# Reordering the first loads and the lead-in of group 0 in a fused two-layer kernel (recurrent attention, gated feed-forward, cross-attention, ternary feed-forward)

## The chip, the cores and the metric

The kernel runs on one core of one Trainium2 chip. The metric is the device time of one execution in microseconds (us); lower is better. The engines are PE (TensorE matmul; PEld is its weight load), DVE (VectorE), ACT (ScalarE), POOL (GpSimd) and SP (SyncE, which here only issues DMAs). Each engine runs its own instructions in program order and waits on semaphores for the others. A name with a q behind it in the profile (SPq, ACTq, POOLq) is the engine's sequencer, which issues DMAs.

## The reference

Sixteen sequences of 128 rows by 256 features pass through four residual stages; the first one is what the change touches.

```python
x = x + mlstm(layernorm(x), ctx, ctx, igate_w, igate_b, fgate_w, fgate_b, ln_scale)   # stage A
x = x + swiglu_ffn(layernorm(x), w_gate, w_up, w_down)                                # stage B
x = x + cross_attention(layernorm(x), ctx, mask, W, diagonal)                         # stage C
x = x + ternary_ffn(layernorm(x), w1, w2, h1, h2, w3)                                 # stage D

def mlstm(q, k, v, ...):                       # 8 heads of 32 features
    ifg = concatenate([q, k, v], axis=-1)
    ig, fg = (ifg @ igate_w.T + igate_b).T, (ifg @ fgate_w.T + fgate_b).T
    cs = cumsum(log_sigmoid(fg), axis=1)
    log_D = where(tril, cs[:, :, None] - cs[:, None, :], -inf) + ig[:, None, :]
    max_log_D = max(log_D, axis=-1, keepdims=True)
    C = (q k^T per head / sqrt(32)) * exp(log_D - max_log_D)
    normalizer = maximum(abs(C.sum(-1)), exp(-max_log_D))
    h = (C / (normalizer + 1e-6)) @ v
    return layernorm(h over all 256 features) * ln_scale
```

## The kernel before, in words

The sixteen sequences are worked on in four groups of four (`G` = 4, `Q` = 4; a group has 512 rows, `GT`). Each engine has one hand-written program: the order of its instructions is the order of the source, and semaphores tie the programs together. Stage A is a loop over the groups in which each group has eight units (four sequences by two sets of four heads, the "quads"). Before the loop stands the lead-in of group 0, which is what the change reorders. Later groups have their own lead-in inside the loop, one group ahead; the loop body is untouched but for one wait.

The lead-in of group 0 goes as follows, by the names in the code.

- SP issues the loads: `x` (group 0, semaphore `x_first`), `graw` (the raw gate weights, `gw_ld`), `kstA` (the transposed context of group 0, `ctxT_ld`), `idf` (an identity matrix, `ident_ld`), small constants (`consts`), and `x` of group 1 (`x_second`).
- DVE computes the statistics of `x` (`x_stats`), POOL the inverse root of the variance (`inv_root`, line 412, semaphore `rstd_ready`), DVE the normalised `xn` (`x_norm`, line 1096). PE transposes `xn` into PSUM (`turn_x`, line 558). Each f32 operand is then split into a rounded high part and a rest: ACT writes the high part of `xT` (`x_hi`, line 889) and of `kT` (`k_hi`, line 893), DVE the low parts (`x_lo`, line 1103, and its own `k_lo`, line 1108). POOL has a `k_lo` as well (line 431), which the loop and the later stages use.
- POOL clears `gw`, `Qb` and `V` (memsets, lines 404 to 408) and builds the split gate weights `gw` from `graw` (lines 417 to 425, semaphore `gw_lo`). `gsum` is the sum of the weights for k and for v.
- PE computes the gates (`gates`, lines 564 to 566, twelve matmuls of 512 columns: six from `kT`, which wait for `klo_done` and `gw_lo`, then six from `xT`). ACT copies them to `gsb` (`gate_copy`, line 897, semaphore `gate_copied`). Two DMAs bring them into `gi` and `gf`, one row per head and sequence.
- DVE and ACT form log-sigmoid, running sum, running minimum and the three bf16 pieces `zp` of the result (`gate_a`, ACT's `log_part`, `gate_b`, ACT's `floor_part`, `gate_c`; semaphore `z_ready` at line 1148). Six DMAs move the pieces into the rows of `Rr` and `Lr`; each adds 16 to `z_moved`.
- The loop on PE opens with `expo` (line 603), which waits for all six (`MOVES` = 96), then `qk` with `Qb`, which SP fills from `xT` (`queries_in`, line 283, four DMAs for each sequence). `V` is filled by four DMAs (`values`, line 273) after the memsets have counted `const_set` to 3. POOL's weight loads for stage B (line 439 on) wait for `z_moved` too.

In the kernel before, SP issues `V`, then `gi`, `Qb`, `x` of groups 2 and 3 and the three `Rr` moves, while ACT issues `gf` and the three `Lr` moves. Line 244 and 245 (`move_rows`) are the form that the loop uses for the later groups, where SP issues all six:

```python
def move_rows(sp, u):
    for part in range(3):
        sp.dma_start(Rr[part:part + 1, u, :, :, :, :], zp[:, part, 0, :]).then_inc(s["z_moved"], 16)
        sp.dma_start(Lr[3 + part * Q:3 + part * Q + Q, u, :, :, :], zp[:, part, 1, :])\
            .then_inc(s["z_moved"], 16)
```

Of the kernel before, what the change touches and what calls it, by code (L numbers as in the profile page):

```python
# [24 lines left out]
NH, DH = 8, 32  # L25
KD = D // P
Q = 4
G = NB // Q
GT = Q * S
# [31 lines left out]
class Chain:  # L61
# [5 lines left out]
    def step(self, ins):  # L67
        ins.then_inc(self.sem, 1)
        self.n += 1
# [18 lines left out]
def two_layers(nc, x_in, ctx_in, ctxT_in, mask_in, gw_in, gb_in, lns_in, l0gu_in, l0d_in, xaw_in, diag_in,  # L88
# [17 lines left out]
    with es:  # L106
# [145 lines left out]
        def _(sp):  # L252
            sp.dma_start(x[:, 0:Q, :], x_in[0:Q].rearrange("b s d -> s b d")).then_inc(s["x_first"], 16)
            sp.dma_start(graw[:, :, :], gw_in).then_inc(s["gw_ld"], 16)
            sp.dma_start(kstA[:, :, :], ctxT_in[:, :, 0:GT]).then_inc(ctxT_ld[0], 16)
            sp.dma_start(idf[:, :], ident_in).then_inc(s["ident_ld"], 16)
            sp.dma_start(gb[:, :], gb_in).then_inc(s["consts"], 16)
# [4 lines left out]
            sp.dma_start(tri[:, :, :], tri_in).then_inc(s["consts"], 16)  # L262
            sp.dma_start(x[:, Q:2 * Q, :], x_in[Q:2 * Q].rearrange("b s d -> s b d")).then_inc(s["x_second"], 16)
            sp.dma_start(lns[:, :], lns_in.partition_broadcast(P)).then_inc(s["consts"], 16)
# [4 lines left out]
            sp.dma_start(kstA[:, :, :], ctxT_in[:, :, GT:2 * GT]).then_inc(ctxT_ld[1], 16)  # L269

            def values(g, u):
                for q in range(Q):
                    sp.dma_start(V[:, u, q, 0:NH, 0:DH],
                                 ctx_in[Q * g + q].rearrange("t (h d) -> t h d", d=DH)).then_inc(v_ld[u], 16)
# [26 lines left out]

            sp.wait_ge(s["const_set"], 3)
            values(0, 0)
            sp.wait_ge(s["gate_copied"], 1)
            sp.dma_start(gi[:, :], gsb[0:NH, :].rearrange("h (q t) -> h q t", q=Q)).then_inc(s["gate_moved"], 16)
            queries_in(0, 0, 0)
            for g in range(2, G):
                sp.dma_start(x[:, Q * g:Q * g + Q, :], x_in[Q * g:Q * g + Q].rearrange("b s d -> s b d"))\
                    .then_inc(s["x_rest"], 16)
            sp.wait_ge(s["z_ready"], 1)  # L310
            for part in range(3):
                sp.dma_start(Rr[part:part + 1, 0, :, :, :, :], zp[:, part, 0, :]).then_inc(s["z_moved"], 16)
            queries_in(0, 0, 1)
            with sp.Fori(0, 2) as i:
# [79 lines left out]
        def _(pool):  # L394
            own = [0]

            def step(ins):
                ins.then_inc(s["pool_own"], 1)
                own[0] += 1

            def settle():
                pool.wait_ge(s["pool_own"], own[0])
# [4 lines left out]

            nc.gpsimd.memset(V[:, :, :, :, :], 1.0).then_inc(s["const_set"], 1)

# [3 lines left out]

            settle()
            inv_root(0)
            pool.wait_ge(s["gw_ld"], 16)
            step(nc.gpsimd.tensor_tensor(gsum[:, :, :], graw[:, KD:2 * KD, :], graw[:, 2 * KD:3 * KD, :], ALU.add))
            settle()
            W = 2 * NH
# [8 lines left out]
            def k_lo(n, kst, u):  # L428
# [3 lines left out]
                    .then_inc(s["klo_done"], 1)  # L432

            inv_root(1)
            pool.wait_ge(s["z_moved"], MOVES)

# [442 lines left out]
        def _(act):  # L879
# [45 lines left out]
            gate_copy(0, QK)  # L925
            act.wait_ge(s["gate_copied"], 1)
            act.dma_start(gf[:, :], gsb[NH:2 * NH, :].rearrange("h (q t) -> h q t", q=Q)).then_inc(s["gate_moved"], 16)
            k_hi(1, kstA[:, :, :], 1)
            x_hi(1, 1)
            log_part(0)  # L930
            floor_part(0)
            act.wait_ge(s["z_ready"], 1)
            for part in range(3):
                act.dma_start(Lr[3 + part * Q:3 + part * Q + Q, 0, :, :, :], zp[:, part, 1, :])\
                    .then_inc(s["z_moved"], 16)
            with act.Fori(0, 2) as i:
# [128 lines left out]
        def _(dve):  # L1065
# [39 lines left out]

            def k_lo(n, par):
                dve.wait_ge(s["khi_done"], n + 1)
                v.tensor_tensor(kT[:, par, 1, :, :], kstA[:, :, :], kT[:, par, 0, :, :], ALU.subtract)\
                    .then_inc(s["klo_done"], 1)

            A2 = 9
# [114 lines left out]
            v.tensor_copy(idb[:, :], idf[:, :]).then_inc(s["idb_ready"], 1)  # L1226
            k_lo(0, 0)
            x_lo(0, 0)
# [7 lines left out]
            x_lo(1, 1)  # L1236
            k_lo(1, 1)
            floor_copy(0, 0)
            with dve.Fori(0, 2) as i:
                for u in range(2):  # L1240
# [6 lines left out]
                    for q in range(Q):  # L1247
# [3 lines left out]
                        if q == 0:  # L1251
                            def close():
                                finish(last, 1 - u, Q - 1, norm=True)
                            before(close)

                            if u == 0:
                                dve.wait_ge(s["pv_used"], Q * g + 1)
                                dve.wait_ge(s["x_rest"], 16 * (G - 2))
                                x_stats(g + 2, 8 - 8 * i)
                            else:  # L1260
                                more(lambda: x_stats(3, 3 * Q))
# [232 lines left out]
```

## Time and profile before

| what | us |
|---|---|
| median of 3 runs | 616.87 (616.14 to 617.22) |
| the profiled execution | 617.22 |
| its span in the trace | 615.7 |
| PE busy | 557.8 (91%) |
| DVE busy | 352.0 (57%) |
| ACT busy | 213.9 (35%) |
| POOL busy | 89.0 (14%) |
| first matmul of stage A's loop | 28.55 after the start |

All times of a row are counted from the start of the span. A timeline row has the start, the length, the engine and line, what it writes and reads, and in brackets how long the engine had been idle before it and what ended that idle time. Where a row merges several instructions, xN is their count and the length is from the first's start to the last's end. A row that tells "DMA to landing" counts from the issue of a DMA to the moment at which its data has landed and its semaphore says so.

### The profile page before, as it was taken

To read this page: it belongs to the slowest core of one execution; us is meant where nothing else is said; L and a number is where in the kernel's file an instruction comes from. 1 tells how busy PE (TensorE), PEld (TensorE's weight loads), DVE (VectorE), ACT (ScalarE), POOL (GpSimd) and SP (SyncE) were. 2 spreads that over 40 slices of the span, in tenths; PEclk is the share of its full clock that TensorE was granted. 3 is DMA by queue.
4 is the path that set the end of the run, shared out by engine and by line. 5 is a ranking of instruction groups with operands and counts; after the bars stand their busy time and mean duration, and the time that the engine had idled before them with its cause. 6 is when DMAs were issued, how large, how long until landed. Compare 5 with 4: busy or idle time off the path is not lost.

```text
span 615.7 us, 8969 instructions
## 1 busy us (share of the span) xinstructions
PE 557.8 (91%) x2728; PEld 452.8 (74%) x2728; DVE 352.0 (57%) x853; ACT 213.9 (35%) x372; POOL 89.0 (14%) x110
## 2 busy tenths in 40 slices
PE   3397988887899999979999999999999999999994
PEld 3164665566788887757888888888878888888884
DVE  6468899877777777865424345344363434542232
ACT  2223142242666663334411236112162222441120
POOL 5114343233300023310000010000100000100001
PEclk9588979886899999988999999999999999999998
DMA  7565444525954739830000000000000000000000
GB/s 202 123 164 150 105 118 78 140 85 189 341 215 149 192 70 353 175 96 1 1 0 2 0 35 1 0 2 0 27 9 0 0 0 0 34 0 0 0 0 34
DMA packets 57752, 47.57 MB, mean 77 GB/s; under 512 B 37278, under 2 KB 48542, under 8 KB 57316
## 3 DMA queue, kind: packets, MB, share of 16 engines
q1 hardware_dynamic: 51960, 28.29, 17.8%
q0 software_dynamic: 5616, 18.88, 9.3%
q8 instruction: 15, 0.25, 0.2%
q14 instruction: 13, 0.11, 0.1%
q10 hardware_dynamic: 148, 0.04, 0.0%
HBM read 40.58 MB, written 2.10 MB: 69 GB/s over the span
## 4 chain that ended last, share of the span: by engine, by line
PE 69%; DVE 4%; issue 2%; ACT 2%; DVEq 0%; POOL 0%; ACTq 0%; POOLq 0%
PE ps L794 52%; PE ps L570 6%; PE ps L573 3%; PE ps L572 2%; PE ps L558 2%; DVE xn L1096 1%; PE ps L765 1%; PE ps L564 1%; ACT al L1024 1%; PE ps L566 1%; PE ps L565 1%; PE ps L779 1%; PE ps L626 0%; ACT h L1059 0%; DVE sc L1344 0%
## 5 line engine op out<-in xcount | busy, mean ns | idle before, releaser
L794 PE MATMUL ps<-hBt,h 128*128 128x512 f32 x512 | 117.4, 390 | 0.0
L794 PE MATMUL ps<-hA,h 128*128 128x512 f32 x512 | 117.2, 390 | 0.0
L794 PEld LDWEIGHTS ps<-hA,h 128*128 128x128 f32 x512 | 95.9, 188 | 20.2 <-DVE hA L1390 0.4
L794 PEld LDWEIGHTS ps<-hBt,h 128*128 128x128 f32 x512 | 95.8, 188 | 20.2 <-DVE hBt L1390 0.4
L1059 ACT ACTIVATE h<-ps,scol 128x512 f32<-128x512 f32 x64 | 44.1, 690 | 175.4 <-PE ps L794 175.3
L794 PE MATMUL ps<-xT,w 128*128 128x512 f32 x256 | 60.7, 397 | 0.2 <-issue 0.2
L794 PEld LDWEIGHTS ps<-xT,w 128*128 128x128 f32 x256 | 46.8, 190 | 13.4 <-DVE h L1385 2.5
L1405 DVE CAST hBt<-h 128x512 fp32r<-128x512 f32 x32 | 13.7, 427 | 73.7 <-ACT h L1059 73.7
L1405 DVE CAST hA<-h 128x512 fp32r<-128x512 f32 x32 | 13.7, 427 | 70.1 <-ACT h L1059 70.1
L412 POOL TENSOR_TENSOR rstd<-ve,mhalf 128x4 f32<-128x4 f32 x16 | 16.4, 1023 | 251.0 <-DVE ve L1091 251.0
L570 PE MATMUL ps<-xT,l 128*128 128x512 f32 x96 | 40.5, 421 | 4.7 <-issue 2.7
L573 PE MATMUL ps<-xT,l 128*128 128x512 f32 x96 | 40.0, 416 | 0.0
L1044 ACT ACTIVATE silD<-ps,scol 128x512 f32<-128x512 f32 x32 | 22.0, 688 | 50.6 <-PE ps L794 50.6
L1385 DVE SCALAR_TENSOR_TENSOR h<-ps,scol,silD 128x512 f32<-128x512 f32 x32 | 24.0, 751 | 24.0 <-ACT silD L1044 24.0
L539 POOL DMA_DIRECT2D out<-x x16 | 8.8, 553 | 178.1 <-DVE x L1416 178.1
L558 PE MATMUL ps<-idf,xn 128*128 128x128 f32 x128 | 18.9, 296 | 14.3 <-DVE xn L1096 14.3
L946 ACT ACTIVATE Dt<-ps 128x512 f32<-128x512 f32 x32 | 19.0, 595 | 35.1 <-PE ps L605 33.8
L1096 DVE TENSOR_SCALAR xn<-x,mv,rstd 128x256 f32 (+1 forms) x64 | 27.1, 486 | 5.0 <-POOL rstd L412 4.7
L889 ACT ACTIVATE xT<-ps 128x512 fp32r<-128x512 f32 x32 | 17.3, 593 | 35.4 <-PE ps L558 35.4
L558 PEld LDWEIGHTS ps<-idf,xn 128*128 128x128 f32 x128 | 16.1, 153 | 17.3 <-DMA idf<-ident_in 9.3
L570 PEld LDWEIGHTS ps<-xT,l 128*128 128x128 f32 x96 | 19.6, 204 | 10.0 <-issue 3.0
L570 PE MATMUL ps<-l0d,hB 128*128 128x256 f32 x96 | 24.1, 291 | 1.4 <-DVE x L1315 1.4
(170 smaller groups left out, 931.5 us busy)
## 6 DMA issues: line engine op xcount, KB each, us to landing
looked<-w_all_in SPq DMA_DIRECT2D x16, 704.0 KB, 4.8
h<-w_all_in POOLq DMA_DIRECT2D x16, 512.0 KB, 6.4
V<-ctx_in SPq DMA_DIRECT2D x32, 128.0 KB, 4.4
Qb<-xT SPq DMA_DIRECT2D x64, 64.0 KB, 2.4
w<-w_all_in POOLq DMA_DIRECT2D x3, 1024.0 KB, 6.9
x<-x_in SPq DMA_DIRECT2D x4, 512.0 KB, 4.3
kstA<-ctxT_in SPq DMA_DIRECT2D x4, 512.0 KB, 5.3
kstC<-ctxT_in SPq DMA_DIRECT2D x4, 512.0 KB, 5.5
```

Of the source, the lines that this page charges most:

```text
L412: nc.gpsimd.tensor_tensor(rstd[:, :], ve[:, :], mhalf[:, :], ALU.pow).then_inc(s["rstd_ready"], 1)
L558: last = nc.tensor.transpose(ps[:, TR + c, q * S:(q + 1) * S], xn[:, q, c * P:(c + 1) * P], idf[:, :])
L570: mm(o, lhs(0), rhs(0), start=first, stop=False)
L573: return mm(o, lhs(0), rhs(1), start=False, stop=last)
L794: last = mm(o, a, b, start=(k == 0 and p == 0), stop=(k == n_k - 1 and p == 1))
L889: fn(xT[:, par, 0, c, :], tr_bank(c), ACT.Copy).then_inc(s["xhi_done"], 1)
L946: fn(Dt[:, quad, :, :], ps[:, EX + quad, :].rearrange("p (j t) -> p j t", j=Q), ACT.Exp, scale=-1.0).then_inc(s["d_ready"], 1)
L1044: fn(silD[:, m % 2, :], ps[:, 2 + m % 2, :], ACT.Silu, scale=scol[:, 0, m:m + 1])\
L1059: fn(h32[:, m % 2, :], ps[:, 2 + m % 4, :], ACT.Gelu, scale=scol[:, L + 1, m:m + 1])\
L1096: last = v.tensor_scalar(xn[:, q, :], x[:, b0 + q, :], mv[:, q, 0:1], rstd[:, q:q + 1], ALU.subtract, ALU.mult)
L1385: v.scalar_tensor_tensor(out=h32[:, m % 2, :], in0=ps[:, 4 + m % 2, :], scalar=scol[:, 1, m:m + 1], in1=silD[:, m % 2, :], op0=ALU.mult, o ...
L1405: v.tensor_copy(dst[:, 0, m, :], h32[:, m % 2, :]).then_inc(s["dh_own"], 1)
```

## The change

The line numbers of the changed kernel are a little lower, since it is shorter. What it does:

- SP's first loads are in another order: `x`, `idf`, `kstA`, `graw`, `x` of group 1, then the constants.
- POOL adds up `gsum` (which needs `graw`) ahead of the first `inv_root`. It computes the low parts of `kT` for groups 0 and 1, which DVE did; the memset of `V` stands between the two.
- SP's lead-in of group 0 uses the loop's own helpers: `gi` and `gf` together, then `x` of groups 2 and 3, then `V`, `Qb`, and all six moves. It waits for `const_set` ahead of `gi`. ACT issues no DMA any more.
- On ACT, `log_part(0)` stands ahead of the `x_hi` of group 1.
- DVE waits for `x_rest` once ahead of the loop, not in it.

```diff
@@ sync (SP)
             sp.dma_start(x[:, 0:Q, :], x_in[0:Q].rearrange("b s d -> s b d")).then_inc(s["x_first"], 16)
+            sp.dma_start(idf[:, :], ident_in).then_inc(s["ident_ld"], 16)
+            sp.dma_start(kstA[:, :, :], ctxT_in[:, :, 0:GT]).then_inc(ctxT_ld[0], 16)
             sp.dma_start(graw[:, :, :], gw_in).then_inc(s["gw_ld"], 16)
-            sp.dma_start(kstA[:, :, :], ctxT_in[:, :, 0:GT]).then_inc(ctxT_ld[0], 16)
-            sp.dma_start(idf[:, :], ident_in).then_inc(s["ident_ld"], 16)
+            sp.dma_start(x[:, Q:2 * Q, :], x_in[Q:2 * Q].rearrange("b s d -> s b d")).then_inc(s["x_second"], 16)
             sp.dma_start(gb[:, :], gb_in).then_inc(s["consts"], 16)
...
-            sp.dma_start(x[:, Q:2 * Q, :], x_in[Q:2 * Q].rearrange("b s d -> s b d")).then_inc(s["x_second"], 16)
...
-
+            sp.wait_ge(s["const_set"], 3)
...
-            sp.wait_ge(s["const_set"], 3)
-            values(0, 0)
-            sp.wait_ge(s["gate_copied"], 1)
-            sp.dma_start(gi[:, :], gsb[0:NH, :].rearrange("h (q t) -> h q t", q=Q)).then_inc(s["gate_moved"], 16)
-            queries_in(0, 0, 0)
+            gates_in(0)
             for g in range(2, G):
                 sp.dma_start(x[:, Q * g:Q * g + Q, :], x_in[Q * g:Q * g + Q].rearrange("b s d -> s b d"))\
                     .then_inc(s["x_rest"], 16)
-            sp.wait_ge(s["z_ready"], 1)
-            for part in range(3):
-                sp.dma_start(Rr[part:part + 1, 0, :, :, :, :], zp[:, part, 0, :]).then_inc(s["z_moved"], 16)
-            queries_in(0, 0, 1)
+            lead_in(0, 0)
@@ gpsimd (POOL)
-            nc.gpsimd.memset(V[:, :, :, :, :], 1.0).then_inc(s["const_set"], 1)
+            pool.wait_ge(s["gw_ld"], 16)
+            step(nc.gpsimd.tensor_tensor(gsum[:, :, :], graw[:, KD:2 * KD, :], graw[:, 2 * KD:3 * KD, :], ALU.add))
+            settle()
...
-            settle()
             inv_root(0)
-            pool.wait_ge(s["gw_ld"], 16)
-            step(nc.gpsimd.tensor_tensor(gsum[:, :, :], graw[:, KD:2 * KD, :], graw[:, 2 * KD:3 * KD, :], ALU.add))
-            settle()
...
+            k_lo(0, kstA[:, :, :], 0)
+            nc.gpsimd.memset(V[:, :, :, :, :], 1.0).then_inc(s["const_set"], 1)
             inv_root(1)
+            k_lo(1, kstA[:, :, :], 1)
             pool.wait_ge(s["z_moved"], MOVES)
@@ scalar (ACT)
             gate_copy(0, QK)
-            act.wait_ge(s["gate_copied"], 1)
-            act.dma_start(gf[:, :], gsb[NH:2 * NH, :].rearrange("h (q t) -> h q t", q=Q)).then_inc(s["gate_moved"], 16)
             k_hi(1, kstA[:, :, :], 1)
+            log_part(0)
             x_hi(1, 1)
-            log_part(0)
             floor_part(0)
-            act.wait_ge(s["z_ready"], 1)
-            for part in range(3):
-                act.dma_start(Lr[3 + part * Q:3 + part * Q + Q, 0, :, :, :], zp[:, part, 1, :])\
-                    .then_inc(s["z_moved"], 16)
@@ vector (DVE)
-            k_lo(0, 0)
             x_lo(0, 0)
...
-            k_lo(1, 1)
             floor_copy(0, 0)
+            dve.wait_ge(s["x_rest"], 16 * (G - 2))
...
-                                dve.wait_ge(s["x_rest"], 16 * (G - 2))
```

On SP, from the second load of `kstA` to the moves of the pieces, before the change (a name on the left of the arrow is written, one on the right is read; L is the line, xN a count):

```order
L269 DMA kstA<-ctxT_in 128x2x512 [waits klo_done]
L273 DMA V<-ctx_in 128x8x32 [waits const_set]
L273 DMA V<-ctx_in 128x8x32 x3
L305 DMA gi<-gsb 32x1x128 [waits gate_copied]
L283 DMA Qb<-xT 32x4x128 [waits qk_done,xhi_done,xlo_done]
L283 DMA Qb<-xT 32x4x128 x3
L308 DMA x<-x_in 128x4x256 x2
L312 DMA Rr<-zp 1x32x128 [waits z_ready]
L312 DMA Rr<-zp 1x32x128 x2
```

The same stretch of SP after the change:

```order
L269 DMA kstA<-ctxT_in 128x2x512 [waits klo_done]
L290 DMA gi<-gsb 32x1x128 [waits gate_copied,const_set]
L291 DMA gf<-gsb 32x1x128
L304 DMA x<-x_in 128x4x256 x2
L273 DMA V<-ctx_in 128x8x32 x4
L283 DMA Qb<-xT 32x4x128 [waits qk_done,xhi_done,xlo_done]
L283 DMA Qb<-xT 32x4x128 x3
L244 DMA Rr<-zp 1x32x128 [waits z_ready]
L245 DMA Lr<-zp 4x8x128
L244 DMA Rr<-zp 1x32x128
L245 DMA Lr<-zp 4x8x128
L244 DMA Rr<-zp 1x32x128
```

Four `V` loads that stood ahead of the wait for `gate_copied` now stand behind it, and four moves more (`gf` and the three `Lr`) are SP's; the last `Lr` follows the twelfth row.

On POOL, from the last memsets to the second inverse root, before the change:

```order
L406 MEMSET Qb 128x2048
L408 MEMSET V 128x2640
L412 ISA
L412 TENSOR_TENSOR rstd<-ve,mhalf 128x4 [waits mv_ready,pool_own]
L417 TENSOR_TENSOR gsum<-graw 128x32 [waits gw_ld]
L420 CAST gw<-graw 128x2x16 [waits pool_own]
L421 CAST gw<-gsum 128x2x16
L423 TENSOR_TENSOR gw<-graw,gw 128x2x16 [waits pool_own]
L425 TENSOR_TENSOR gw<-gsum,gw 128x2x16
L412 TENSOR_TENSOR rstd<-ve,mhalf 128x4 [waits mv_ready]
```

The same stretch of POOL after the change:

```order
L399 MEMSET Qb 128x2048
L402 ISA
L402 TENSOR_TENSOR gsum<-graw 128x32 [waits gw_ld]
L407 TENSOR_TENSOR rstd<-ve,mhalf 128x4 [waits mv_ready,pool_own]
L411 CAST gw<-graw 128x2x16
L412 CAST gw<-gsum 128x2x16
L414 TENSOR_TENSOR gw<-graw,gw 128x2x16 [waits pool_own]
L416 TENSOR_TENSOR gw<-gsum,gw 128x2x16
L422 TENSOR_TENSOR kT<-kstA,kT 128x1024 [waits khi_done]
L426 MEMSET V 128x2640
L407 TENSOR_TENSOR rstd<-ve,mhalf 128x4 [waits mv_ready]
L422 TENSOR_TENSOR kT<-kstA,kT 128x1024 [waits khi_done]
```

The wait for the load of `graw` moved ahead of the first inverse root, and two subtractions of 128 by 1024 for `kT` were added.

## Rows read from the trace of the kernel before

**Rows 1.** Waits from 0 to 30 us: total us, times, longest
```profile
POOL l L439 <- DMA Lr<-zp: 12.3, 1, 12.3
```

**Rows 2.** Timeline, 2.7 to 16 us: start, length, engine, line [idle before]
```profile
2.75 0.59 SPq L256 DMA_DIRECT2D idf<-ident_in  x1
...
6.77 1.04 POOL L412 TENSOR_TENSOR rstd<-ve,mhalf 128x4 f32<-128x4 f32 x1 [0.81 <-DVE ve L1091]
...
7.79 0.24 POOL L417 TENSOR_TENSOR gsum<-graw 128x32 f32<-128x32 f32 x1
7.84 1.38 DVE L1096 TENSOR_SCALAR xn<-x,mv,rstd 128x256 f32<-128x256 f32 x4 [1.23 <-POOL rstd L412]
...
8.72 0.28 POOL L423 TENSOR_TENSOR gw<-graw,gw 128x32 fp32r<-128x32 f32 x1
8.97 1.63 POOL L425 TENSOR_TENSOR gw<-gsum,gw 128x32 fp32r<-128x32 f32 x1
...
9.27 1.22 DVE L1108 TENSOR_TENSOR kT<-kstA,kT 128x1024 fp32r<-128x1024 f32 x1
...
10.96 0.78 PE L564 MATMUL ps<-kT,gw 128*128 128x512 f32 x1
...
15.63 0.59 ACT L897 ACTIVATE gsb<-ps 16x512 f32<-16x512 f32 x1 [3.20 <-PE ps L566]
```

**Rows 3.** DMA issues from 0 to 40 us: count, KB each, median us to landing
```profile
idf<-ident_in SPq DMA_DIRECT2D x1, 64.0 KB, 5.8
graw<-gw_in SPq DMA_DIRECT2D x1, 48.0 KB, 3.1
```

**Rows 4.** POOL's own k_lo in the loop, line 431: min/median/max ns
```profile
L431 POOL TENSOR_TENSOR kT<-kstA,kT x2: 2365/2370/2374, 60.2 to 89.6; 128x1024 fp32r<-128x1024 f32 x2
```

**Rows 5.** Timeline of the sequencers and the loop's first matmul, 10 to 29 us
```profile
10.52 0.56 SPq L269 DMA_DIRECT2D kstA<-ctxT_in  x1
...
11.12 3.95 SPq L273 DMA_DIRECT2D V<-ctx_in  x4
...
16.24 0.86 SPq L305 DMA_DIRECT2D gi<-gsb  x1
...
17.23 2.61 SPq L283 DMA_DIRECT2D Qb<-xT  x4
...
19.89 1.54 SPq L308 DMA_DIRECT2D x<-x_in  x2
...
25.07 2.04 ACTq L934 DMA_DIRECT2D Lr<-zp  x3
...
28.55 0.60 PE L603 MATMUL ps<-Rr,Lr 15*128 15x512 bf16 x1 [1.82 <-DMA Lr<-zp]
```

**Rows 6.** The third of the four V issues alone, timeline of SP
```profile
12.49 1.88 SPq L273 DMA_DIRECT2D V<-ctx_in  x1
```

**Rows 7.** Landing of line 269 (kstA), then of line 308 (x): min/median/max
```profile
DMA to landing us min/median/max: 4.0/4.0/4.0
...
DMA to landing us min/median/max: 3.6/4.3/5.0
```

**Rows 8.** Timeline in the loop, group 1, where SP issues everything
```profile
50.16 0.56 SPq L244 DMA_DIRECT2D Rr<-zp  x1
...
53.84 0.68 SPq L245 DMA_DIRECT2D Lr<-zp  x1
```

**Rows 9.** Timeline, the gate chain of group 0 on DVE and ACT
```profile
18.78 0.28 DVE L1116 TENSOR_SCALAR fmn<-gf,gb 32x128 f32<-32x128 f32 x1 [0.97 <-DMA gf<-gsb]
...
20.85 0.29 ACT L902 ACTIVATE fl<-fab 32x128 f32<-32x128 f32 x1
```

**Rows 10.** Timeline in the loop, POOL and DVE side by side
```profile
45.10 1.79 POOL L454 TENSOR_TENSOR l<-rawgu,l  x1
45.23 1.80 DVE L1138 TENSOR_TENSOR Er<-Z,cs 32x128 f32<-32x128 f32 x1
```

**Rows 11.** Windows, 28.5 to 35 us: busy of each engine, PE's granted clock, DMA
```profile
28.50:35.00 6.50, 6.45 (x15) 3.99 (x16) 2.34 (x6) 1.19 (x2) 2.35 (x4) 0.50 0.88 265
```

More of the change, by code:

```diff
@@ L1104, in x_lo @@
                         .then_inc(s["xlo_done"], 1)
[L1106 to L1109, printed above, removed]
             A2 = 9
```

## The prediction, made before the changed kernel ran

> **What bounds the kernel now.** I read the waits of the first 30 us, then the timeline up to the loop's first matmul, then the DMA landings. PE carries the kernel from the loop's opening on, and the loop opens at 28.55, when the last `Lr` move has landed [rows 5]. POOL's weight loads for stage B wait for the same moves, 12.3 us [rows 1], and every later load waits for work of the loop or behind it. So nothing behind the opening runs by a time of its own: a shift of the opening shifts the end by as much. The change leaves the loop body alone; the whole question is when the loop opens.
>
> Three points lie on the way to it. R is the end of the first inverse root: 6.77 + 1.04 = 7.81. T is the end of the gate copy: 15.63 + 0.59 = 16.22. The opening comes 28.55 - 16.22 = 12.33 after T [rows 2, 5].
>
> **R: the wait for graw stands ahead of the root.** POOL now needs `graw` before the root. `graw` is issued fourth, in the place that `idf` had: issue at 2.75, behind the 512 KB of `kstA`. `idf` landed 5.8 later, at 8.55; `graw`, second in line before, landed after 3.1 [rows 2, 3]. By the place in the queue it lands at 8.55; the sum of the weights (0.24) and the root (1.04) then give R = 9.9 with the gaps: **+2.1**. If it kept its 3.1 it would land at 5.9, before the statistics are ready at 6.77, and R would not move: the other end is 0. I take 2.1, since the size is like that of `idf` (48 and 64 KB) and the place is the same. The Trainium skill, "DMA: Bandwidth & Descriptors", section "Queues, rings and completion order", says that each DMA engine consumes the descriptors of one ring in order, though a later one may finish its write first; the row of `idf` agrees with the first half, and by the second half alone the term could be nearer to 0.
>
> **From R to T: the low part of kT on POOL.** Before, PE started the gates at 10.96, which is R + 3.15: DVE's `k_lo` took 1.22 and ran beside POOL's work on `gw`. Now POOL does both in a row. Its own `k_lo` takes 2.37 [rows 4] and can't start before the `gw` splits are through. From R to the start of the last split were 8.97 - 7.81 = 1.16, less 0.24 for the sum, which has gone ahead: 0.92. The last split took 1.63 where its twin took 0.28, and it ended at 10.60, just behind DVE's `k_lo` (9.27 to 10.49) [rows 2]. I read it as held up by DVE, so with that work gone it costs 0.28, once DVE's `xn` is through at R + 1.41. Then: R + 1.44 + 0.28 + 2.37 + 0.36 (10.60 to 10.96, release to matmul) = R + 4.45, or **+1.3**. Ends: 0.92 + 0.28 + 2.37 + 0.36 = 3.93, +0.8; and with 1.63 as the split's own price 0.92 + 1.63 + 2.37 + 0.36 = 5.28, +2.1. The Trainium skill, "SBUF — State Buffer", section "SBUF: two separate sides", has VectorE and GpSimd share a pair of ports as an exclusive lock, which a VectorE instruction with two SBUF inputs takes against a GpSimd one; the pair 0.28 and 1.63 agrees. By that rule the term is 1.3, and without it 2.1.
>
> The `xT` side is no later than that: it moves with R and is ready at 13.3 + 2.1 = 15.4, when PE is still at its six `kT` matmuls (from 14.3 on). I leave the twelve matmuls and the way to the copy at 15.63 - 10.96 = 4.67. T comes at 16.22 + 2.1 + 1.3 = 19.6, **+3.4**.
>
> **From T to the opening: SP's queue.** Two things have to be there: `z_ready`, and SP. `z_ready` gains. It came at 25.05, T + 8.8. ACT's exp ran at 20.85 behind `x_hi(1)`, though `fab` had been ready at about 19.4 [rows 9]; `log_part` now stands ahead: -1.5. `gf` goes behind `gi` on SP, 0.86 + 0.68 against 1.33 on ACT's queue: +0.2. That makes T + 7.6.
>
> SP is later. From T it issues `gi` 0.86, `gf` 0.68 (the price of a move of the same queue [rows 8]), `x` twice 1.54, `V` 3.95 and `Qb` 2.61 [rows 5]: T + 9.65. Only `gi`, `Qb` and `x` stood there before, and `V` was issued from 11.12 to 15.07, where SP had nothing else to do. The `V` price may grow. Three of the four issues are near 0.66, and the third took 1.88, up to 14.37 [rows 6], which is when the 512 KB of `kstA` that stood ahead (10.52 + 4.0) landed [rows 5, 7]. Now 1 MB of `x` stands ahead: its second half, issued at about T + 2.3, lands at T + 7.3 by the 5.0 of [rows 7]. If the third `V` issue is again held till then, the fourth and `Qb` bring SP to T + 7.3 + 0.66 + 2.61 = T + 10.6. Without any stall it is T + 8.4. I take T + 10.2, between the row as it stands and the longer one.
>
> Then all six moves go out from one queue, where ACT and SP shared them (ACT's three took 2.04). In the loop the six span 50.16 to 54.52, 4.36, of which their own durations are about 3.7 [rows 8]; I take 4.0. The last lands 28.55 - 27.11 = 1.44 later [rows 5]. The opening is at T + 10.2 + 4.0 + 1.44 = T + 15.6, **+3.3** against 12.33. Ends: T + 8.4 + 3.7 + 1.44 = 13.5, +1.2; T + 10.6 + 4.4 + 1.44 = 16.4, +4.1, and 1.5 more if a second `V` issue is held.
>
> **What costs nothing, and its cover.** The memset of `V` (2.3) is behind `k_lo(0)` and ends near 16.5, before T. The second root waits for it, and `xn` of group 1 is done by about 20; it is wanted only for `x_lo(1)`, behind the gate chain. The second load of `kstA` is issued at 14 instead of 10.5 and lands at 18, before T. DVE loses its second `k_lo`, 1.2, which was off the way; POOL's second one, 2.4 from about T + 1.1, may hold the gate chain: in the loop a 32 by 128 instruction of DVE took 1.80 beside POOL's 1.79 [rows 10], where others of its size take 0.28 [rows 9]. SP's slack of 10.2 - 7.6 = 2.6 covers that; without the slack it would cost up to 1.5. The wait for `x_rest` on DVE is met at about T + 7.3, before DVE gets there. Behind the opening all stands as before: `Qb` of the second sequence follows the moves, and `V` lands long before its first use.
>
> **Sum.** 2.1 + 1.3 + 3.3 = 6.7. The profiled execution took 617.22 (span 615.7 and 1.5 around it), so it would take 623.9. The median of the three is 0.35 lower: **623.6**.
>
> **Rivals.**
> (a) `graw` lands early. For it: its 3.1 of before. Against: the row of `idf`. 6.7 - 2.1 = 4.6: 621.5.
> (b) SP is not what the opening waits for; the gate chain is. It decides where SP is through `Qb` by T + 7.6, which asks for issues 2 us shorter than those of [rows 5]. T + 7.6 + 4.0 + 1.44 = T + 13.0, +0.7; with 3.4 it gives 4.1: 621.0. With (a) too: 618.9.
> (c) The queues stall more: several `V` issues are held behind 1 MB of `x`, or the moves land late behind 4,096 small `V` rows and `Qb`, and the last split costs 1.63. 2.1 + 2.1 + 4.1 + 1.5 = 9.8: 626.7.
> (d) The opening is not what sets the end: some later transfer, started by a time of its own, ends the slack. I find none; it would give 616.9.
> (e) Faster: PE's clock. It is granted half speed in the first 6.5 us of the loop, with PE busy for 6.45 [rows 11]. Were it at full speed from the opening, these would take half, -3.2; with the least shift of the lead-in (0 + 0.8 + 1.2 = 2.0) that is -1.2: 615.7. It decides at a granted clock of 1.0 at the opening. Against it: PE has been idle ahead of the opening, as before, and for longer.
>
> **Chances and range.** A run of this kernel can tell about 0.2%, 1.2 us, from no change. My forecast with terms near their values 0.50; (a) 0.17; (b), with or without (a), 0.11; (c) 0.14; (d) 0.04; (e) 0.04. Slower by over 0.2% are the first four but for a rest of (b) with (a): 0.90. Within it: 0.06. Faster: 0.04. The range goes from 619.3, above the case of (a) with (b), to 626.8, where (c) is taken in.
>
> **What would show it.** POOL's `gsum` at about 8.6 and the root's end near 9.9 (step one; at 6.1 and 7.8 it is wrong). POOL's `k_lo` ending near 14, with a last split of 0.3, PE's first gate matmul at 14.3 (step two). The gate copy ending at 19.6. The third `V` issue stalled till `x` lands, `z_ready` 2 us before SP takes it, six moves in 4 us, and the loop's first matmul near 35.2 (step three). From there on the same distance to the end, 587 us. I would be wrong altogether if that distance changed by over 1 us.

## The result, and the profile after

The changed kernel took 621.88 us (median of 6 runs, 620.58 to 624.29) against 616.5 for the kernel before (614.6 to 617.51, 6 runs). The ratio is 1.0109, with a 95% interval from 1.0078 to 1.0141: about 1% slower. It rests on more runs than the two medians do (22 of the changed kernel, whose median is 623.0), so it is not their quotient. All ratios leave out executions over 1.5% longer than the shortest of the same kernel; for a_guard and a_fix these are five of before's 19. The span of the profiled execution went from 615.7 to 622.1, +6.4. The forecast was 623.6, +6.7. The sum was close, but not by its own steps: the loop opened 9.5 later, not 6.7, and the loop gave 3.1 back, which I had forecast at nothing.

The first view is the timeline of the changed kernel, POOL, DVE and the first gate matmul, in the stretch that [rows 2] shows of before (start, length, engine, line, operands, idle before):

```profile
9.53 0.24 POOL L402 TENSOR_TENSOR gsum<-graw 128x32 f32<-128x32 f32 x1 [5.82 <-DMA graw<-gw_in]
9.86 1.04 POOL L407 TENSOR_TENSOR rstd<-ve,mhalf 128x4 f32<-128x4 f32 x1
...
10.93 3.43 DVE L1084 TENSOR_SCALAR xn<-x,mv,rstd 128x256 f32<-128x256 f32 x4 [4.32 <-POOL rstd L407]
...
11.50 0.30 POOL L416 TENSOR_TENSOR gw<-gsum,gw 128x32 fp32r<-128x32 f32 x1
11.76 2.45 POOL L422 TENSOR_TENSOR kT<-kstA,kT 128x1024 fp32r<-128x1024 f32 x1
14.16 2.44 POOL L426 MEMSET V<- 128x2640 f32 x1
...
14.28 2.40 DVE L1209 CAST idb<-idf 128x128 bf16<-128x128 f32 x1
...
16.78 0.77 PE L558 MATMUL ps<-kT,gw 128*128 128x512 f32 x1 [0.33 <-issue]
...
21.59 0.59 ACT L891 ACTIVATE gsb<-ps 16x512 f32<-16x512 f32 x1 [4.01 <-PE ps L560]
```

Two things are to be seen. POOL waits 5.82 for `graw`, and the root ends at 10.90 instead of 7.81. Then `xn`, four instructions of DVE, takes 3.43 instead of 1.38, and the cast of `idb` 2.40 instead of 0.2. Both end just when an instruction of POOL does: `xn` at 14.36 behind `k_lo` (14.21), the cast at 16.68 behind the memset (16.60). One line of the source view shows that one of the four instructions took all of it (min, median, max in ns):

```profile
L1084 DVE TENSOR_SCALAR xn<-x,mv,rstd x4: 399/421/2424, 10.9 to 11.9; 128x256 f32<-128x256 f32 x4
```

The landing of `graw`, from the view of DMA issues that [rows 3] shows of before:

```profile
graw<-gw_in SPq DMA_DIRECT2D x1, 48.0 KB, 6.7
```

The second stretch goes from the gate copy (T = 22.18) to the opening of the loop, on SP and DVE, as [rows 5, 6, 9] do of before:

```profile
23.93 0.99 SPq L304 DMA_DIRECT2D x<-x_in  x2
24.97 4.96 SPq L273 DMA_DIRECT2D V<-ctx_in  x4
...
29.76 0.41 DVE L1131 TENSOR_TENSOR zp<-zr,zp 32x256 bf16<-32x256 f32 x1
30.04 2.74 SPq L283 DMA_DIRECT2D Qb<-xT  x4
...
32.82 0.60 SPq L244 DMA_DIRECT2D Rr<-zp  x1
...
36.08 0.67 SPq L245 DMA_DIRECT2D Lr<-zp  x1
...
38.07 0.60 PE L597 MATMUL ps<-Rr,Lr 15*128 15x512 bf16 x1 [6.20 <-DMA Lr<-zp]
```

`zp` is ready at 30.17, T + 8.0, and SP is through `Qb` at 32.78, T + 10.6: the moves wait for SP, not for their data. The third `V` issue alone, from the timeline of SP, took 2.40. It ended at 28.75, and the second half of `x`, issued at 24.42, landed 4.5 later, at 28.9:

```profile
26.35 2.40 SPq L273 DMA_DIRECT2D V<-ctx_in  x1
```

The third stretch is the opening of group 1. First before (the last move, issued at 53.84, is in [rows 8]), then after the change: SP's last moves, POOL's first weight load, and PE's first matmul of the group.

```profile
53.23 0.56 SPq L244 DMA_DIRECT2D Rr<-zp  x1
53.74 0.72 POOL L439 DMA_DIRECT2D l<-l0gu_in  x1
...
57.80 0.38 PE L603 MATMUL ps<-Rr,Lr 15*128 15x512 bf16 x1 [2.30 <-DMA Lr<-zp]
```

```profile
62.39 0.54 SPq L244 DMA_DIRECT2D Rr<-zp  x1
...
62.97 0.67 SPq L245 DMA_DIRECT2D Lr<-zp  x1
63.30 0.72 POOL L433 DMA_DIRECT2D l<-l0gu_in  x1
...
64.98 0.39 PE L597 MATMUL ps<-Rr,Lr 15*128 15x512 bf16 x1
```

Before, POOL's load was issued 0.10 ahead of the last move, that move landed about 3.3 after its issue had ended, and PE waited 2.30. After, the move was issued 0.33 ahead of the load, and PE did not wait. The windows around it show what followed (busy of PE, PEld, DVE, ACT, POOL, then PE's granted clock, DMA share and GB/s), before and after:

```profile
57.80:66.50 8.70, 8.70 (x38) 6.29 (x38) 5.67 (x18) 2.14 (x3) 3.12 (x3) 0.80 0.73 219
```

```profile
65.00:72.50 7.50, 7.45 (x39) 5.28 (x38) 7.11 (x22) 3.00 (x5) 3.55 (x4) 1.00 0.80 246
```

Behind the wait PE had a granted clock of 0.80 on average, without it 1.00, over nearly the same matmuls. So 2.3 came back at the opening of group 1 and 1.2 in the first two units behind it (9.5 late at the loop's opening, 7.2 at that of group 1, 6.0 two units further). At the later units the changed kernel is mostly 6.0 to 6.5 behind (7.6 at the most), and at the end of the span 6.4.

### The profile page after: what moved, and what is told of

It is laid out like the page before. It is cut to its first block, busy times and chain, and to the rows that moved or that the text cites. A ratio compares the mean times of both kernels' runs of the same rounds, so it can differ in the third digit from the quotient of the medians.

```text
span 622.1 us, 8968 instructions
## 1 busy us (share of the span) xinstructions
PE 555.4 (89%) x2728; PEld 449.4 (72%) x2728; DVE 354.3 (57%) x851; ACT 213.4 (34%) x372; POOL 92.4 (15%) x112
## 4 chain that ended last, share of the span: by engine, by line
PE 67%; DVE 3%; issue 2%; ACT 1%; POOL 0%; DVEq 0%; ACTq 0%; POOLq 0%
PE ps L788 51%; PE ps L564 5%; PE ps L567 3%; PE ps L566 2%; PE ps L552 2%; DVE xn L1084 1%; PE ps L759 1%; PE ps L558 1%; PE ps L560 1%; ACT al L1012 1%; PE ps L559 1%; PE ps L773 1%; ACT h L1047 0%; DVE sc L1325 0%; DVE x L1296 0%
## 5 line engine op out<-in xcount | busy, mean ns | idle before, releaser
L1084 DVE TENSOR_SCALAR xn<-x,mv,rstd 128x256 f32 (+1 forms) x64 | 29.2, 518 | 7.8 <-POOL rstd L407 7.8
```

Of the source, the lines that this page charges most:

```text
L1084: last = v.tensor_scalar(xn[:, q, :], x[:, b0 + q, :], mv[:, q, 0:1], rstd[:, q:q + 1], ALU.subtract, ALU.mult)
```

## The experiments

An opening is read from one profile each. It is told as a distance, since the first landings and PE's clock moved the gate copy of the five kernels with before's loads and POOL from 16.07 to 17.37, and what lies behind stage A varied by 6.6 between profiles (482.4 and 482.5 in before and after, 479.4 to 486.0 in others). R is the end of the first root, T the end of the gate copy. Each ratio is to the runs of before that were taken with that kernel, whose medians were 616.5 to 617.6. The profile of a_split is of an execution of 624.79, 5.5 above its median, so only its lead-in and the distance to group 1 are read.

| kernel | R | gates start - R | T | opening - T | group 1 - opening | total, median | ratio to before |
|---|---|---|---|---|---|---|---|
| before | 7.81 | 3.15 | 16.22 | 12.33 | 29.25 | 616.5 | |
| after | 10.90 | 5.88 | 22.18 | 15.89 | 26.91 | 621.88 | 1.0109 (1.0078 to 1.0141) |
| a_graw | 7.81 | 4.27 | 17.62 | 16.07 | 26.89 | 620.67 | 1.0047 (1.0021 to 1.0074) |
| a_klo_dve | 11.25 | 5.34 | 21.50 | 15.98 | 27.19 | 622.03, one run | |
| a_vmem | 10.26 | 5.20 | 20.10 | 15.89 | 27.06 | 621.59, one run | |
| a_split | 11.30 | 5.88 | 22.18 | 13.06 | 29.36 | 619.32 | 1.0044 (1.0013 to 1.0075) |
| a_vfirst | 9.79 | 5.88 | 21.31 | 13.22 | 26.68 | 618.13, one run | |
| a_guard | 10.26 | 7.44 | 22.35 | 15.89 | 27.09 | 618.73 | 1.0072 (1.003 to 1.0115) |
| a_fix | 7.86 | 4.76 | 18.65 | 13.23 | 26.93 | 613.04 | 0.9985 (0.9935 to 1.0036) |
| b_onequeue | 7.82 | 4.71 | 17.19 | 13.33 | 26.81 | 612.24, one run | |
| b_log | 7.81 | 3.52 | 16.70 | 10.90 | 28.70 | 615.63 | 0.9978 (0.9942 to 1.0013) |
| b_guard | 7.81 | 4.09 | 16.07 | 11.95 | 27.28 | 611.85 | 0.9927 (0.9897 to 0.9957) |
| b_both | 7.81 | 4.85 | 17.37 | 11.15 | 28.39 | 611.54 | 0.9902 (0.9869 to 0.9935) |

The column "gates start - R" says something of before itself. Up to the gates its program is that of b_onequeue, b_log, b_guard and b_both, and yet it has 3.15 where they have 3.52 to 4.85: in them `idf` landed 6.4 to 7.8 after its issue, and `kstA` 6.8 to 8.1, instead of 5.8 and 6.0. So before's profile shows its lead-in at the fast end, and against those four the way from R to T grew by 1.7 to 3.0, not by 2.9.

**POOL's work holds up DVE: three runs.** The first moves `graw` ahead, so that `xn` is over when POOL's long instructions begin.

```diff
             sp.dma_start(x[:, 0:Q, :], ...)
-            sp.dma_start(idf[:, :], ident_in)...
-            sp.dma_start(kstA[:, :, :], ctxT_in[:, :, 0:GT])...
             sp.dma_start(graw[:, :, :], gw_in)...
+            sp.dma_start(kstA[:, :, :], ctxT_in[:, :, 0:GT])...
+            sp.dma_start(idf[:, :], ident_in)...
```

> The changed kernel with graw issued second again and idf fourth. Theory 1 (two terms: graw's place in the queue, and POOL's work in SBUF holding up DVE): the root ends at 7.8 instead of 10.9, xn then runs from 7.8 to 9.2, ahead of POOL's k_lo, which starts when k_hi is through at about 10.2, so xn takes 1.4 and not 3.4; the gates start near 12.9, the gate copy ends near 18.3, the loop opens at 34.2 instead of 38.07 (-3.9). Rival (xn was long for another reason, such as the loads landing beside it): only graw's own 3.1 comes back, the loop opens near 35.0 and xn stays at 3.4. Total near 618.

Its timeline:

```profile
6.77 1.04 POOL L407 TENSOR_TENSOR rstd<-ve,mhalf 128x4 f32<-128x4 f32 x1 [1.82 <-DVE ve L1079]
...
7.84 1.41 DVE L1084 TENSOR_SCALAR xn<-x,mv,rstd 128x256 f32<-128x256 f32 x4 [1.22 <-POOL rstd L407]
...
9.18 0.21 DVE L1209 CAST idb<-idf 128x128 bf16<-128x128 f32 x1
...
9.59 2.35 POOL L422 TENSOR_TENSOR kT<-kstA,kT 128x1024 fp32r<-128x1024 f32 x1 [0.87 <-ACT kT L887]
11.88 2.30 POOL L426 MEMSET V<- 128x2640 f32 x1
```

Every point came out as the first theory had it: the root at 7.81, `xn` 1.41, the gate copy at 17.62 (18.3 was expected), the opening at 33.69 (34.2). The late `graw` costs its own 3.1 and, through the place in which it puts `xn`, 1.6 more between R and the gates (5.88 to 4.27). The total is 620.67, ratio 1.0047 where the changed kernel had 1.0109: about 3.8 of the 4.4 by which the opening came sooner, as far as these intervals tell (they nearly touch).

The second takes `k_lo` from POOL and leaves the memset of `V` where the change put it.

```diff
@@ gpsimd
-            k_lo(0, kstA[:, :, :], 0)
             nc.gpsimd.memset(V[:, :, :, :, :], 1.0)...
             inv_root(1)
-            k_lo(1, kstA[:, :, :], 1)
@@ vector
+            k_lo(0, 0)      # behind the cast of idb, as before
+            k_lo(1, 1)      # behind x_lo(1, 1), as before
```

> The changed kernel with both k_lo of the lead-in back on DVE; POOL's memset of V stays where it is, so that it now follows the gw splits at once (about 11.8 to 14.2). Theory 1 (POOL's work in SBUF holds up DVE, a memset too): xn still takes about 3.4 and the gate copy still ends at 21.5 to 22.2. Rival (what cost was the length of POOL's k_lo in the chain of the gates): xn takes 1.4, the gates start 2.7 earlier, the gate copy ends near 19.5.

```profile
11.28 3.57 DVE L1082 TENSOR_SCALAR xn<-x,mv,rstd 128x256 f32<-128x256 f32 x4 [4.67 <-POOL rstd L407]
...
12.10 2.29 POOL L425 MEMSET V<- 128x2640 f32 x1
...
14.78 0.21 DVE L1212 CAST idb<-idf 128x128 bf16<-128x128 f32 x1
```

With no `k_lo` on POOL at all `xn` still takes 3.57, and its long instruction (2.57) ends at 14.5, behind a memset now. So the length of POOL's subtraction in the chain of the gates, which my step priced, was not what cost.

The third puts only the memset back ahead of everything.

```diff
             nc.gpsimd.memset(Qb[:, 0, :, :, :, :].bitcast(F32), 0.0)...
+            nc.gpsimd.memset(V[:, :, :, :, :], 1.0).then_inc(s["const_set"], 1)
             pool.wait_ge(s["gw_ld"], 16)
...
             k_lo(0, kstA[:, :, :], 0)
-            nc.gpsimd.memset(V[:, :, :, :, :], 1.0).then_inc(s["const_set"], 1)
```

> The changed kernel with the memset of V ahead of everything, as before the change. Theory 1: xn is still held by POOL's k_lo (3.4), but the cast of idb is not held by the memset (0.2 instead of 2.4), so the gates start 0.7 earlier, at 16.1, and the gate copy ends at 21.5 instead of 22.2. Rival (the cast was long for its own reasons): no change, 22.2.

```profile
10.29 3.43 DVE L1084 TENSOR_SCALAR xn<-x,mv,rstd 128x256 f32<-128x256 f32 x4 [3.67 <-POOL rstd L408]
...
11.13 2.45 POOL L423 TENSOR_TENSOR kT<-kstA,kT 128x1024 fp32r<-128x1024 f32 x1
13.65 0.21 DVE L1209 CAST idb<-idf 128x128 bf16<-128x128 f32 x1
```

`xn` as long as ever behind `k_lo`, the cast back at 0.21, the gates 0.7 sooner against R (5.20 against 5.88), as expected. T came 1.4 sooner than that, 20.10: `graw` had landed 0.6 earlier in this execution, and the gates ran at the higher clock sooner.

These three settle it: 2.05 for `xn` and 0.7 for the cast make up the 2.7 between R and the gates. The other profiles agree: `xn` took 3.43 to 5.67 in all six with `graw` fourth, and 1.38 or 1.41 in all seven with it second. The page of the Trainium skill that I cited, "SBUF — State Buffer", section "SBUF: two separate sides", names both sorts of VectorE instruction that take the shared ports, those with two SBUF inputs and those in a two-port performance mode. The traces agree with the second half, which I had left out: `xn` and the cast have one SBUF input each, and were held to the end of POOL's instruction. No trace shows the mode in which an instruction ran, and not every one was held: DVE's statistics of `x` took 1.33 beside the early memset of `V` in before and 1.33 without it in the changed kernel, and `x_lo`, which reads PSUM, took 1.29 beside the memset in a_graw and 1.29 in before.

**SP's queue behind the gate copy: three runs.** The first gives the lead-in of group 0 its old division back.

```diff
@@ sync
+            values(0, 0)          # ahead of the wait for gate_copied
+            ... gi, queries_in(0, 0, 0), x of groups 2 and 3, three Rr moves, queries_in(0, 0, 1)
-            gates_in(0)
-            ... x of groups 2 and 3
-            lead_in(0, 0)
@@ scalar
+            ... gf behind gate_copy(0), three Lr moves behind floor_part(0)
```

> The changed kernel with the lead-in of group 0 dealt out to SP and ACT as before the change (V ahead of the wait for the gate copy, gf and the three Lr moves on ACT); loads, POOL and the place of log_part as changed. Theory 2 (SP's queue sets the opening): the gate copy ends at 22.2 as in the changed kernel, z_ready is at T + 7.4, the moves leave in 2.0, the loop opens at T + 10.9 = 33.1 instead of T + 15.9. Rival (the landing of x and V sets it, not the issuing): it opens within 1 us of 38. For the total the opening is 5 earlier, so 616.9 if nothing is given back in the loop, 619 to 620 if what the loop gave back (3.1 at the opening of group 1) belongs to the late opening.

The opening came at T + 13.06, not T + 10.9, and not T + 15.9 either. SP's queue is 2.8 of the way, and something new took 2.1 of what was expected:

```profile
24.73 2.34 POOL L428 TENSOR_TENSOR kT<-kstA,kT 128x1024 fp32r<-128x1024 f32 x1 [2.78 <-ACT kT L893]
24.74 2.40 DVE L1111 TENSOR_SCALAR fmn<-gf,gb 32x128 f32<-32x128 f32 x1 [1.37 <-DMA gf<-gsb]
```

POOL's second `k_lo` started 0.01 ahead of the first instruction of the gate chain and held it for 2.40 instead of 0.28. The prediction had this case, at up to 1.5, under the cover of SP's slack. In the changed kernel the cover held (`fmn` 0.32 at 25.30); here, with SP ready, it had gone. The total is 619.32, where 619 to 620 was expected for the case that the late opening is what makes the loop give back; b_guard, below, shows that it is not. Group 1 opened 29.36 behind the loop, as in the kernel before: nothing was given back.

The second run moves only the `V` loads ahead of the wait and leaves all moves on SP.

```diff
+            values(0, 0)
             gates_in(0)
             ... x of groups 2 and 3
-            lead_in(0, 0)
+            queries_in(0, 0, 0)
+            sp.wait_ge(s["z_ready"], 1)
+            move_rows(sp, 0)
+            queries_in(0, 0, 1)
```

> The changed kernel with the four V loads ahead of the wait for the gate copy on SP, all six moves still on SP. Theory 2 in its parts: SP is through Qb at about T + 6, z_ready at T + 7.6 decides, the moves leave in 3.9 and land 1.4 later, so the loop opens at T + 12.9, 3.0 earlier against T than in the changed kernel (T + 15.9), and of the 3.6 that the lead-in grew behind T the V loads are 3.0 and the moves the rest. Rival (the second half of x, not V, holds SP and the moves): it opens at T + 15 or later.

```profile
15.52 2.93 SPq L273 DMA_DIRECT2D V<-ctx_in  x4
...
34.53 0.60 PE L601 MATMUL ps<-Rr,Lr 15*128 15x512 bf16 x1 [3.53 <-DMA Lr<-zp]
```

The opening is at T + 13.22 (12.9 expected). `V` behind the gate copy costs 2.7. Issued ahead of the gate copy, 1.8 after the 512 KB of `kstA` had been issued, the four take 2.93 and none is held.

The third starts from the kernel before and moves only `gf` and the three `Lr` moves to SP.

```diff
@@ sync
             sp.dma_start(gi[:, :], ...)
+            sp.dma_start(gf[:, :], ...)
...
                 sp.dma_start(Rr[part:part + 1, 0, :, :, :, :], ...)
+                sp.dma_start(Lr[3 + part * Q:3 + part * Q + Q, 0, :, :, :], ...)
@@ scalar
-            ... gf and the three Lr moves
```

> The kernel before with gf and the three Lr moves issued by SP, all else as before: the price of one queue alone. Theory 2: the six moves leave in 3.9 instead of 2.04 and gf lands about as before, so the loop opens 1.9 later, at 30.4. Rival (the landing sets the opening, not the issuing): 28.6.

```profile
30.52 0.60 PE L606 MATMUL ps<-Rr,Lr 15*128 15x512 bf16 x1 [3.56 <-DMA Lr<-zp]
...
57.33 0.39 PE L606 MATMUL ps<-Rr,Lr 15*128 15x512 bf16 x1
```

The opening came at 30.52 (30.4 expected), but 1.0 of it is a later T. Against T it is 13.33, +1.0: the moves take 3.9 instead of 2.0, and the chain ahead of them is 0.7 shorter, since ACT does not stand in the issue of `gf` (`z_ready` at T + 8.1 instead of T + 8.8). What I had not expected is group 1: it opened 26.81 behind the loop, and PE had no wait for `Lr`. With the kernel before's loads and POOL, 2.4 came back. So this part of the change costs 1.0 at the opening and brings more: its one run took 612.24, less than each of the 29 runs of before beside it (612.93 to 622.26), and in its profile the last unit of stage A starts 4.2 sooner than in before's.

**What the loop gave back: five runs.** Four of them try the order of the last move and POOL's loads. The guard is one wait more, in the loop of POOL:

```diff
                     if u == 0:
+                        pool.wait_ge(s["z_moved"], MOVES * (gn + 1))
                         pieces(i, 1)
                     else:
                         with pool.If(i < 1):
+                            pool.wait_ge(s["z_moved"], MOVES * (gn + 1))
                             pieces(1, 0)
```

> The kernel before with one wait more: in the loop POOL issues its weight loads for stage B only when the six moves of the next group have landed. Theory 3 (the last Lr move lands late since POOL's loads are already in the DMA engines; PE waits 2.3 for it at the opening of group 1 and then loses about 1 more at the half clock): group 1 opens at about 55.5 instead of 57.80 and the fourth unit behind it is 3.4 earlier; the loop's opening stays at 28.55. Total 3 lower, 614. Rival (the late opening of the changed kernel is what gave the 3 back, by other loads being through): no gain, group 1 opens at 57.8.

```profile
52.92 0.68 SPq L245 DMA_DIRECT2D Lr<-zp  x1
53.73 2.57 SPq L283 DMA_DIRECT2D Qb<-xT  x4
...
55.30 0.38 PE L605 MATMUL ps<-Rr,Lr 15*128 15x512 bf16 x1 [0.73 <-DMA Lr<-zp]
55.88 0.62 POOL L439 DMA_DIRECT2D l<-l0gu_in  x1 [3.01 <-DMA Lr<-zp]
```

Group 1 opened at 55.30 (55.5 expected); PE's wait fell from 2.30 to 0.73, the distance from 29.25 to 27.28, and from the second unit behind it on the units start 3.7 sooner (3.4 expected; 0.5 of it was there at the loop's opening). The total is 611.85, 0.9927 of before (0.9897 to 0.9957), more than the 3 expected. The rival, that the give-back belongs to the late opening, falls: here the loop opened early and the time came back too.

Why did the last move leave 0.4 later, and so behind POOL's load, in some kernels? In all profiles with before's SP program (before, a_split, b_log, b_guard, b_both) SP leaves 0.45 empty between the fourth and the fifth move of group 1; in all with a longer one (the changed kernel and the rest of its family that keep six moves on SP, b_onequeue) it does not. Nothing that the profile shows ends that gap. So the give-back goes with the length of SP's program, which the change happened to raise by four DMA issues; what makes the gap itself stays open.

The next run is the one part of the change that should gain, alone.

```diff
-            x_hi(1, 1)
             log_part(0)
+            x_hi(1, 1)
```

> The kernel before with log_part(0) ahead of x_hi(1) on ACT, alone. Theory: the exp runs at 19.4 instead of 20.85, z_ready and the moves come 1.5 earlier, the loop opens at 27.1. Rival (x_hi(1), now later, holds x_lo(1) and with it the opening): 28.5 or more. Total 1.5 lower if nothing in the loop takes it back.

The opening is at T + 10.90 instead of 12.33: 1.4 of the 1.5. The total is 615.63, ratio 0.9978 (0.9942 to 1.0013), which the timing can't tell from no change. Its profile has one thing more. PE waited 1.91 at group 1, and the windows behind that wait show the full clock, where before's showed 0.80:

```profile
56.30:64.00 7.70, 7.70 (x40) 5.66 (x41) 6.59 (x17) 2.42 (x4) 3.14 (x3) 1.00 0.66 201
```

So only the wait itself was lost there. Then both together:

> The kernel before with both: log_part first and POOL's loads behind the moves. If the two gains are apart and both hold, 4.5 to 5 lower than before, 612.5; the loop opens at 27.1 and group 1 at 54. Rival (stage A gives one of them back at a later group): 614 to 616.

The total is 611.54, ratio 0.9902 (0.9869 to 0.9935): the best of this study, by a little, and ahead of both kernels. Its interval overlaps with that of the guard alone. The loop opened at 28.52 and group 1 at 56.91, where 27.1 and 54 were expected. T was 1.15 later than in before, at 17.37, and against T the opening kept its gain (11.15). The distance to group 1 is 28.39, less than half of the guard's gain there; in this execution PE's granted clock was 0.61 in the 4.5 ahead of group 1 (its sixteen `V` matmuls there took 3.71, against 2.02 in the changed kernel).

> The changed kernel with POOL's loads in the loop behind the moves, as in b_guard. Theory 3: at group 1 there is nothing to win, since the moves land in time there already (distance from the loop's opening to that of group 1 stays at 26.9), but the late Qb landing of group 3 (between 120 and 135 us) goes, about 5. Total 617. Rival (the changed kernel has no such wait left): 622.

The changed kernel with the guard: 618.73 (617 expected), ratio 1.0072 (1.003 to 1.0115). That interval overlaps with the changed kernel's own. The distance to group 1 stays (27.09), as expected, since there was nothing to win. The wait in group 3 went, as expected (below), and the last unit of stage A starts 4.9 sooner than in the changed kernel. In this profile the long instruction of `xn` was not let in between `k_lo` and the memset, as it was in the changed kernel: it took 4.66, held through both, and `xn` 5.67.

The last run undoes two parts of the change and adds the guard: `graw` second, `V` first.

> The changed kernel with graw issued second, V ahead of the gate copy's wait, and POOL's loads in the loop behind the moves. By theories 1 to 3: gate copy ends at 17.6, the loop opens at 30.5, group 1 near 57.4, nothing late in group 3: total 612.5, as the kernel before with log_part first and the same guard (611.5). Rival (the pieces are not apart, POOL's k_lo still costs elsewhere): 615 or more.

613.04, ratio 0.9985 (0.9935 to 1.0036): 612.5 was expected. The opening is at T + 13.23, T at 18.65, 1 later than expected. It can't be told from before. Two pieces that cost in the lead-in are left in it: `k_lo` on POOL ahead of the gates, and six moves on one queue (1.0 at the opening).

**Group 3, half open.** PE waits 1.8 for `Qb` in group 3 of the kernel before, has a granted clock of 0.53 in the next 7.0, and two units there take 9.5; the changed kernel has the same (2.0, 0.54 and 9.5).

```profile
120.51 0.80 PE L564 MATMUL ps<-Qb,kT 128*128 128x512 f32 x1 [1.84 <-DMA Qb<-xT]
```

The wait is there in all nine profiles without the guard, and its size sorts them: at 1.8 to 2.1 (before, after, a_graw, b_log) the two units take 9.5, at 0.3 to 1.3 (the other five) 4.7 to 6.1. In the four with the guard there is none, and they take 4.4 to 4.8. So the guard goes with its absence, four of four against none of nine, and this is the part of its gain that the opening of group 1 does not explain. How a guard on POOL's loads reaches the `Qb` loads of SP was not tried by a run of its own. Some 3 to 5 hang on this wait from one kernel to the next, which is why totals follow the openings so loosely.

## Why the prediction was right, and where it was not

- **What bounds the kernel: the opening of the loop.** Right as to where to look. The sentence that a shift of the opening shifts the end by as much failed, and with it my own sign of being wrong altogether came true, a change of that distance by over 1: it went from 587.1 to 584.0. What I had taken for a fixed body had a race in it, and the timeline behind [rows 8] held it: the last move issued at 53.84, with POOL's first load 0.10 ahead of it. I read that place for the price of six moves, and not for who waited for the last one.
- **R, +2.1.** Measured +3.1, a term mis-sized. The mechanism was right: `graw` in the fourth place landed after 6.7, as `idf` had after 5.8. In the six profiles with `graw` fourth it landed after 5.6 to 7.1, and in the seven with `idf` fourth that landed after 5.8 to 7.8: the same place, the same spread, and the row of before was at its early end. Second in line, either landed after 3.0 to 3.2. Rival (a) fell.
- **From R to T, +1.3.** Measured +2.9, and the wrong mechanism. POOL's `k_lo` did end at 14.2 as foreseen, and the last split took 0.30, as the lock would have it. What the step missed is the other direction: the lock that it used to explain one row of POOL also holds DVE. `xn` lost 2.05 and the cast 0.7. The upper end of the step, 2.1, did not cover it.
- **From T to the opening, +3.3.** Measured +3.56. `z_ready` T + 8.0 against 7.6, SP T + 10.6 against 10.2, six moves 3.93 against 4.0, landing 1.32 against 1.44. The long `V` stall was the one that came true, at 2.40, and ended within 0.2 of the landing of `x`, as the step had it. Rival (b) fell: SP was last by 2.6.
- **What costs nothing.** The second `k_lo` was covered in the changed kernel, and cost 2.1 where a_split took the cover away: the note on it was right, at too low a price. The memset of `V` was called free, and cost 0.7 through the cast.
- **The sum.** 3.1 + 2.9 + 3.6 gives 9.5 at the opening (9.52 before rounding) against 6.7, less 3.1 that the loop gave back. Two errors of about 3 with opposite signs nearly cancelled: that the time came out so near was luck. The step from T to the opening was right; the step from R to T and the fixed distance behind the opening were not.

## What to carry to other kernels

Before moving an instruction to GpSimd because it is idle, lay it over VectorE's timeline: here single GpSimd instructions of 2.3 to 2.45 us, a memset among them, each held the f32 VectorE instruction of 0.2 to 0.4 that ran into them until their end. A DMA queue is a chain like an engine's: a wait put ahead of idle-time loads turns them into path, and a load that a first step needs must not go behind half a megabyte. And a small transfer that opens the next stage should leave ahead of bulk loads by a wait, not by luck.

## What the runs showed of the hardware

- VectorE instructions with one SBUF input were held by GpSimd's: one of `xn` went from 0.4 to 2.42 by a subtraction, to 2.57 by a memset and to 4.66 by both in a row, a cast from 0.2 to 2.40 by a memset, a 32 by 128 instruction from 0.28 to 2.40 by a subtraction. Statistics of `x` (0.4 each) and subtractions that read PSUM (0.65 each) were not held by a memset.
- An 8 KB move landed 1.3 after its issue had ended where the DMA engines were quiet (busy share 0.05), and 3.3 after it where the first of GpSimd's loads of 384 KB had been issued 0.10 ahead (0.87).
- Issuing a DMA from SP stalled where much was queued: the third of four equal loads took 2.40 right behind 1 MB and 1.88 right behind 0.5 MB, and the four 2.93 in all where the 0.5 MB had been issued 1.8 earlier.
- A wait of 2.3 of TensorE cost 3.5: the granted clock averaged 0.80 in the next 8.7 us, against 1.00 without the wait. A wait of 1.9 at the same place in b_log left it at 1.00, one of 1.8 in group 3 was followed by 0.53.
